# Low-rank adapters of a feed-forward layer in two groups of four sequences, with 256-column matmuls and high and low parts of a weight in one block

## The reference, cut to what matters

```python
H, F, RANK, SCALE = 1024, 2752, 16, 0.5
def lora_add(base, inp, A, B):              # A[16, RANK, in], B[16, out, RANK]
    Ab, Bb = A[lora_indices], B[lora_indices]      # one adapter for each sequence
    t = jnp.einsum('bri,bni->bnr', Ab, inp)
    return base + jnp.einsum('bor,bnr->bno', Bb, t) * SCALE
gate = lora_add(jnp.einsum('bnh,fh->bnf', x, W_gate), x, A_gate, B_gate)
up   = lora_add(jnp.einsum('bnh,fh->bnf', x, W_up),   x, A_up,   B_up)
act  = jax.nn.silu(gate) * up
x = x + lora_add(jnp.einsum('bnf,hf->bnh', act, W_down), act, A_down, B_down)
```

## Time and profile before

| | |
|---|---|
| time, median of 3 runs | 2395.77 us (2394.46 to 2396.67) |
| span of the profiled execution | 2393.5 us, from its first to its last instruction |
| what the median has beyond that span | 2.3 us |
| busy share of PE, PE's weight loads, DVE, ACT, POOL | 97%, 80%, 54%, 36%, 4% |
| granted TensorE clock, mean | 0.993 of full speed |
| start of L3 on PE | 701.7 us |
| DMA, mean rate | 172 GB/s; 352 to 354 in most of L1 and L2, 90 to 153 in L3 |

### The profile page before, as it was taken

One profiled execution on the slowest core, in us unless ns is written; L12 is line 12 of the kernel. 1 busy time (PEld: TensorE's weight loads), 2 busy tenths in 40 slices (PEclk: granted clock), 3 DMA queues, 4 the chain that ended last, 5 costly groups with the idle time before them and its releaser, 6 DMA issues.

```text
span 2393.5 us, 31068 instructions
## 1 busy us (share of the span) xinstructions
PE 2315.4 (97%) x10712; PEld 1915.5 (80%) x10712; DVE 1288.3 (54%) x1365; ACT 853.9 (36%) x775; POOL 101.6 (4%) x194
## 2 busy tenths in 40 slices
PE   2998999999989999999999999999999999999997
PEld 2997888788878888887888888788888878888885
DVE  7778999899974433443443345344334534433452
ACT  2214777677753321232332122233212223321221
POOL 4000000000000012000001200000020000000000
PEclk9999999999999999999999999999999999999999
DMA  6988999899953244333324433332442333232231
GB/s 218 337 324 317 353 352 353 307 354 352 352 203 99 97 136 153 99 107 115 99 95 137 153 99 107 115 99 93 139 153 99 107 115 99 90 118 79 99 107 65
DMA packets 127120, 412.42 MB, mean 172 GB/s; under 512 B 16918, under 2 KB 51926, under 8 KB 104918
## 3 DMA queue, kind: packets, MB, share of 16 engines
q1 hardware_dynamic: 115542, 379.32, 45.1%
q0 software_dynamic: 9344, 31.99, 4.1%
q10 hardware_dynamic: 2176, 0.26, 0.1%
HBM read 402.83 MB, written 32.28 MB: 182 GB/s over the span
## 4 chain that ended last, share of the span: by engine, by line
PE 93%; DVE 4%; issue 1%; DVEq 0%; ACT 0%; DMA 0%; POOL 0%; SPq 0%; ACTq 0%
PE ps L1145 24%; PE ps L1147 23%; PE ps L1146 23%; PE ps L1092 6%; PE ps L1094 6%; PE ps L1093 6%; PE ps L1069 3%; PE ps L1102 1%; DVE masked L743 1%; DVE red L702 0%; PE ps L1056 0%; DVE sin L659 0%; DVE mag L696 0%; DVE ang L659 0%; DVE turn L699 0%
## 5 line engine op out<-in xcount | busy, mean ns | idle before, releaser
L940 DVE TENSOR_TENSOR pl<-raw,ph 128x1152 fp32r<-128x1152 f32 (+2 forms) x240 | 343.1, 1430 | 919.0 <-ACT ph L559 919.0
L559 ACT ACTIVATE ph<-raw 128x1152 fp32r<-128x1152 f32 (+2 forms) x240 | 293.9, 1224 | 1172.0 <-PE ps L1147 1172.0
L1145 PE MATMUL ps<-xh,ph 128*128 128x512 f32 x1440 | 561.7, 390 | 8.1 <-DVE xl L958 7.3
L1146 PE MATMUL ps<-xl,ph 128*128 128x512 f32 x1440 | 561.3, 390 | 0.0
L1147 PE MATMUL ps<-xh,pl 128*128 128x512 f32 x1440 | 561.2, 390 | 0.0
L877 DVE TENSOR_TENSOR wl<-W,wh 128x2048 fp32r<-128x2048 f32 x160 | 362.3, 2286 | 29.0 <-ACT wh L501 29.0
L1145 PEld LDWEIGHTS ps<-xh,ph 128*128 128x128 f32 x1440 | 271.0, 188 | 65.6 <-DVE xl L958 7.5
L1147 PEld LDWEIGHTS ps<-xh,pl 128*128 128x128 f32 x1440 | 271.0, 188 | 56.4
L1146 PEld LDWEIGHTS ps<-xl,ph 128*128 128x128 f32 x1440 | 271.0, 188 | 56.2
L1145 PE MATMUL ps<-acth,ph 128*128 128x512 f32 (+1 forms) x792 | 312.5, 395 | 0.0
L1146 PE MATMUL ps<-actl,ph 128*128 128x512 f32 (+1 forms) x792 | 308.4, 389 | 0.0
(11 more groups left out here) (165 smaller groups left out, 1705.8 us busy)
## 6 DMA issues: line engine op xcount, KB each, us to landing
W<-in_w SPq DMA_DIRECT2D x160, 1024.0 KB, 4.9
raw<-in_wgu SPq DMA_DIRECT2D x168, 512.0 KB
toep<-kpad SPq DMA_DIRECT2D x32, 1024.0 KB, 8.1
raw<-in_wd SPq DMA_DIRECT2D x32, 768.0 KB
raw<-in_wd SPq DMA_DIRECT2D x32, 640.0 KB
picked_b<-in_lora_b POOLq DMA_DIRECT2D x32, 352.0 KB, 3.4
raw<-picked_b SPq DMA_DIRECT2D x168, 64.0 KB
urev<-in_urev SPq DMA_DIRECT2D x32, 256.0 KB, 4.1
```

The costliest lines, as they stand in the source:

```text
L559: nc.scalar.activation(ph[:, n % 2, 0:blocks * P], raw[:, n % RAW, 0:blocks * P], ACT.Copy).then_inc(hi_ready, 1)
L940: V.tensor_tensor(out=pl[:, n % 2, 0:blocks * P], in0=raw[:, n % RAW, 0:blocks * P], in1=ph[:, n % 2, 0:blocks * P].bitcast(F32), op=ALU.s ...
L1145: mm(bank(bk), lhsT=wh, rhs=mh, start=first, stop=False)
L1146: mm(bank(bk), lhsT=wh, rhs=ml, start=False, stop=False)
```

## The change

Eight sequences with one adapter block each become two groups of four (`GS` = 4 sequences, `GC` = 256 columns).

- Panels 0 and 1 are no longer gate and up, but group 0 and group 1: in each the rows 0 to 63 of the product are the gate adapters of four sequences and the rows 64 to 127 the up adapters. They run over the 256 columns of their group alone, 24 matmuls each.
- The second matrices take two blocks, one for each group, with the four adapters' 64 ranks in rows 0 to 63 and the same ranks again in rows 64 to 127. ACT rounds all 128 rows to high parts. DVE then puts the low part into rows 64 to 127. `tmh` holds the high part of the small product in both halves, `tml` its low part in rows 0 to 63 and zeros below. Two matmuls of 256 columns for each group (high and low weights x high, high weights x low) do what three of 512 columns did.
- The down adapter's first matrices (`AD0`, `AD1`): `ph` holds for each block of hidden channels the high parts of group 0 (64 columns) beside its low parts (64 columns), `pl` the same of group 1. For each block four matmuls of 256 columns take the place of three of 512. The high and low halves of the product are added later: ACT's `lift_adapter` copies one half down, DVE's `down_adapter` adds, masks and cuts.
- The eight last down panels: the half block of hidden channels (64 rows) and the down adapter's second matrices (64 ranks) share one block for each group. `wdh` holds the half block twice, and `gather` copies it beside the adapters. Nine full blocks are followed by six matmuls of 256 columns with 128 rows, where there were three with 64 rows and three with 128 rows, all of 512 columns.
- `gather` writes the second matrices twice (rows 0 to 63 and 64 to 127) in pieces of one rank, 512 bytes, where it wrote pieces of 8 KB. It issues six DMAs for each sequence and one more for each tile, where it issued five.

Counted in the same way, a tile now has 1536 matmuls of 512 columns and 360 of 256 columns: 48 in panels 0 and 1, 168 in the gate and up panels, 8 in the last one of them, 88 in `AD0` and `AD1`, 48 in the down panels. 294 matmuls of 512 columns are gone.

The diff, cut to its core:

```diff
+GS = TB // 2
+GC = GS * H
-GATHERED = TB * 5 * 16
+GATHERED = (TB * 6 + 1) * 16
@@ POOL, gather
+                    g, s = b // GS, b % GS
                     for k in range(2):
-                        pool.dma_start(lora_a[tile, k, :, b]...
+                        pool.dma_start(lora_a[tile, g, :, k, s]...
-                    pool.dma_start(lora_b[tile, :, b * R:(b + 1) * R].rearrange("t a r w -> (t a) (r w)"),
-                                   ins["lora_b"][one].rearrange("a n r w -> (a n) (r w)")).then_inc(lora_out, 16)
+                    for copy in range(2):
+                        r0 = copy * HALF + s * R
+                        pool.dma_start(lora_b[tile, :, r0:r0 + R, g].rearrange("t a r w -> (t a) r w"),
+                                       ins["lora_b"][one].rearrange("a n r w -> (a n) r w")).then_inc(lora_out, 16)
...
+                pool.dma_start(lora_bd[tile, :, 0:HALF].rearrange("t o r g w -> (t o) (r g w)"),
+                               ins["wdh"].rearrange("o r g w -> o (r g w)")).then_inc(lora_out, 16)
@@ ACT
+            def cut_down_adapter(n, blocks, t):
+                come(n, t)
+                for g, to in enumerate((ph, pl)):
+                    half = nc.scalar.activation(
+                        to[:, n % 2, 0:blocks * P].rearrange("p (k d s r) -> p d s k r", d=2, s=GS, r=R)[:, 0],
+                        raw[...][:, g * GS:(g + 1) * GS], ACT.Copy)
+                half.then_inc(hi_ready, 1)
+            def lift_adapter(t):
+                act.wait_ge(panel_done, t * NPAN + (AD1 + 3))
+                nc.scalar.activation(hid[0][HALF:P], bank(BANK_AD)[0:HALF], ACT.Copy).then_inc(lifted, 1)
...
-                        cut(4 + 2 * k, LT + 1, t, j)
+                        cut(4 + 2 * k, LT + 2, t, j)
@@ DVE
-            def cut(n, blocks, t, j=0):
+            def cut(n, blocks, t, j=0, lora=0):
...
+                if lora:
+                    ranks = slice(blocks * P, (blocks + lora) * P)
+                    main = V.tensor_tensor(out=ph[HALF:P, n % 2, ranks], in0=raw[HALF:P, n % RAW, ranks],
+                                           in1=ph[HALF:P, n % 2, ranks].bitcast(F32), op=ALU.subtract)
+                main.then_inc(lo_ready, 1)
...
+            def adapter(k, g, t):
...
+                V.tensor_tensor(out=part, in0=prod, in1=mask, op=ALU.mult)
+                for copy in range(2):
+                    last = V.tensor_tensor(out=tmh[copy * HALF:(copy + 1) * HALF, k, cols], in0=prod, in1=mask,
+                                           op=ALU.mult)
+                last.then_inc(th_ready, 1)
+                dve.wait_ge(th_ready, t * 7 + (count + 1))
+                V.tensor_tensor(out=tml[0:HALF, k, cols], in0=part, in1=tmh[own, k, cols].bitcast(F32),
+                                op=ALU.subtract).then_inc(t_ready, 1)
+            def down_adapter(t):
+                dve.wait_ge(lifted, t + 1)
...
@@ PE
+            def adapter(g, t):
+                panel_in(g, t)
+                cols = slice(g * GC, (g + 1) * GC)
+                for k in range(LT):
...
+                    last = three(ps[:, BANK_A - g, 0:GC], block_of(ph, g, k), block_of(pl, g, k),
+                                 xh[:, k, cols], xl[:, k, cols], k == 0, k == LT - 1)
+            def panel(n, bk, t, j=0, blocks=LT, at=0, start=True, ranks=(), ready=0):
...
+                for i, c in enumerate(ranks):
+                    for g in range(2):
+                        both = block_of(ph, n, blocks + 2 * i + g)
+                        to, cols = ps[:, bk, g * GC:(g + 1) * GC], slice(g * GC, (g + 1) * GC)
+                        mm(to, lhsT=both, rhs=tmh[:, c, cols], start=False, stop=False)
+                        last = mm(to, lhsT=both, rhs=tml[:, c, cols], start=False, ...)
+            def down_adapter(n, blocks, t, ready, start, stop):
+                panel_in(n, t)
+                for k in range(blocks):
+                    if k in ready:
+                        pe.wait_ge(act_ready, ready[k])
+                    for g, both in enumerate((ph, pl)):
...
+                        mm(to, lhsT=block_of(both, n, k), rhs=acth[:, k, cols], start=first, stop=False)
+                        last = mm(to, lhsT=block_of(both, n, k), rhs=actl[:, k, cols], start=False, stop=end)
+            def down(n, o, blocks, t, shared=False):
...
+                if shared:
+                    pe.wait_ge(t_ready, t * 5 + 5)
+                    for g in range(2):
+                        to, cols = ps[:, DOWN[o % 3], g * GC:(g + 1) * GC], slice(g * GC, (g + 1) * GC)
+                        last = three(to, block_of(ph, n, blocks + g), block_of(pl, n, blocks + g),
+                                     acth[:, blocks, cols], actl[:, blocks, cols], False, g == 1)
```

More of the change, by code:

```diff
@@ L368, in _ @@
                         sp.wait_ge(lora_out, ((t + 1) % NTILE + 1) * GATHERED)
-                    load(AD1 + 1 + o, lora_bd[bass.ds(t, 1), o].rearrange("t p w -> (t p) w"),
-                         at=F1 * P, incs=16)
+                    load(AD1 + 1 + o, lora_bd[bass.ds(t, 1), o].rearrange("t p g w -> (t p) (g w)"),
+                         at=(F1 - 1) * P, incs=16)
                 for k in range(2):
@@ L1035, in _ @@
                 cut(AD1 + 2, F1 + 1, t)
-                adapter(0, 2, AD1, BANK_AD, t)
+                down_adapter(t)
                 cut_rows((t + 1) % NTILE, t + 2)
@@ L1126, in _ @@
                 turn_product(base - 1, 1)
-            def panel(n, bk, blocks, hi, lo, t, j=0, start=True, stop=True, extra=(), extra_ready=0,
-                      ready=None, sem=act_ready, at=0):
-                pe.wait_ge(lo_ready, t * NPAN + j * 4 + (n + RAW + 1))
-                moving = [(hi[:, at + k], lo[:, at + k]) for k in range(blocks)]
-                moving += [(tmh[:, k], tml[:, k]) for k in extra]
-                for k, (mh, ml) in enumerate(moving):
-                    if extra and k == blocks:
-                        pe.wait_ge(t_ready, t * 3 + extra_ready)
-                    if ready and k in ready:
-                        pe.wait_ge(sem, ready[k])
-                    rows = HALF if hi is acth and n >= AD1 and k == F1 - 1 else P
-                    wh, wl, mh, ml = (a[0:rows] for a in (ph[:, n % 2, k * P:(k + 1) * P],
-                                                          pl[:, n % 2, k * P:(k + 1) * P], mh, ml))
-                    first, end = start and k == 0, stop and k == len(moving) - 1
-                    mm(bank(bk), lhsT=wh, rhs=mh, start=first, stop=False)
-                    mm(bank(bk), lhsT=wh, rhs=ml, start=False, stop=False)
-                    last = mm(bank(bk), lhsT=wl, rhs=mh, start=False, stop=end)
@@ new lines, in panel @@
+            def panel(n, bk, t, j=0, blocks=LT, at=0, start=True, ranks=(), ready=0):
+                panel_in(n, t, j)
+                for k in range(blocks):
+                    last = three(bank(bk), block_of(ph, n, k), block_of(pl, n, k), xh[:, at + k], xl[:, at + k],
+                                 start and k == 0, False)
+                if ranks:
+                    pe.wait_ge(t_ready, t * 5 + ready)
+                for i, c in enumerate(ranks):
[3 more added lines that the diff above has]
+                        mm(to, lhsT=both, rhs=tmh[:, c, cols], start=False, stop=False)
+                        last = mm(to, lhsT=both, rhs=tml[:, c, cols], start=False,
+                                  stop=c == ranks[-1] and g == 1)
@@ L1163, in _ @@
                 done = lambda k: t * FT + (k + 1)
-                panel(AD0, BANK_AD, F0, acth, actl, t, stop=False,
-                      ready={0: done(F0 - 3), F0 - 2: done(F0 - 2), F0 - 1: done(F0 - 1)})
+                down_adapter(AD0, F0, t, {0: done(F0 - 3), F0 - 2: done(F0 - 2), F0 - 1: done(F0 - 1)},
+                             start=True, stop=False)
                 for o in range(LT):
-                    panel(AD0 + 1 + o, DOWN[o % 3], F0, acth, actl, t)
+                    down(AD0 + 1 + o, o, F0, t)
                 with pe.Fori(0, F1 // 2 - 1) as j:
@@ L1171, in _ @@
                 gate_up(0, AD1 - 4, t)
[L1172 to L1176 removed]
+                panel(AD1 - 2, GATE[1], t, blocks=LT // 2)
+                panel(AD1 - 1, GATE[1], t, blocks=LT // 2, at=LT // 2, start=False, ranks=(0, 1), ready=4)
+                down_adapter(AD1, F1, t, {0: done(FT - 3), F1 - 2: done(FT - 2), F1 - 1: done(FT - 1)},
+                             start=False, stop=True)
                 for o in range(LT):
[L1178 to L1179 removed]
+                    down(AD1 + 1 + o, o, F1 - 1, t, shared=True)
 def kernel(**inputs):
```

160 lines of the change are left out of this document (99 added, 61 removed).

## The result

| | median us | lowest to highest | runs |
|---|---|---|---|
| before | 2395.6 | 2394.5 to 2396.7 | 4 |
| after | 2318.3 | 2317.0 to 2319.3 | 4 |

The ratio is 0.9676 (95% interval 0.9664 to 0.9688). The kernel is faster by 77.3 us. 100.8 us were forecast, so 23.5 us are missing.

A forecast was written before the change was run, and what follows sets the result against it. PE's matmul count times start distance was taken to bound L3. Per tile 25.6 + 3.8 - 3.7, times four 102.8, less 2 for the gather: 100.8 us gained, 2295 us forecast, range 2278 to 2335.

The forecast's parts named there:

- the forecast's own share: Whole kernel: the chance of 0.69 given to the forecast itself, counted from 2280 to 2316 us.
- rival C: Waits at short panels twice as long, 512-byte gather pieces at half rate holding up the convolution: 2320 us; chance 0.13.
- main term: L3 on PE: 294 matmuls of 512 columns go, 360 of 256 come, gaining 25.6 us per tile.
- half block: Eight down panels and AD1: no more switching to 64 rows and back, 0.42 us each, gaining 3.8 us per tile.
- I take 0.114: Distance between 256-column matmuls in L3, about half the measured 0.2267 us; 360 of them make 41.0 us.
- upper of the two near bounds: 256-column distance of 0.120 us, if 0.0134 came once per matmul; the whole kernel would be 9 us up.
- floor of 0.109: Lower bound for the 256-column distance, from 128-column transposes with weight loads, eight in 0.87 us.
- those rows lie on the floor: Argument against partly hidden weight loads (distance 0.13 to 0.17, 2318 to 2376 us, chance 0.10), citing plain float32 short matmuls.
- Rival A: Weight loads not hidden by 256-column matmuls: 0.222 us each, some 2437 us in all, slower by 41; chance 0.07.
- I leave it out: Start of AD1: DVE's extra operation in the cut before, some 0.4 us, was given no cost.
- the convolution's own loads can be late by nothing (they are asked for ahead): Lower end of the gather's delay to the convolution, up to 4 us; 2 us was taken, once.
- six of eight sequences are issued by 40 us: Tile 0's gather: only the other quarter and `wdh`, some 4 us, would fall between 40 and 80 us.

The follow-up runs named there:

- experiment 1: The kernel before, with only the half block's three matmuls in AD1 and the last down panels given 128 rows instead of 64: 2381.1 us, ratio 0.9939.
- Experiment 2: The changed kernel, with tile 0's gather spread out: three sequences at the start, five and the half block during L1 and L2: 2317.6 us, ratio 0.9670.
- experiment 7: The changed kernel, with tile 0's copies of the down adapter's matrices and `wdh` made at the start of L3: 2312.2 us, ratio 0.9652.
- experiment 8: The changed kernel with four edits: half block earlier, panel 2's adapter steps first, `hidden` before the next cut, down-panel gather deferred: 2299.8 us, ratio 0.9598, fastest version run.

## Why the prediction was right in sign and 23 us too low

The time is inside the range of 2278 to 2335, at 2318.3, but 2 us above the 2316 up to which the forecast's own share was counted, and near the 2320 of rival C. That rival had the waits grow by 15 us in all and the gather cost 10 us more. Less than half of that came: 4 us more of waits and 6 more for the gather; 3 us at the tile boundaries are in neither. The largest part of what is missing is the spacing of matmuls. The main term's mechanism and the half block held; four terms fell short.

**Spacing of 256-column matmuls: right mechanism, mis-sized by 8%.** "I take 0.114" was the step. Measured, they are 0.118 to 0.120 apart, and the 512-column matmuls behind them in each panel lose another 0.026 in all. For the 360 of a tile that makes 0.1228 each and 360 x 0.0088 = 3.2 us per tile more than forecast. The upper of the two near bounds, 0.0134 us per matmul on top of one column per cycle, was the right reading at 256 columns: it gives 0.120. (At 128 it would give 0.067, where three of four distances are 0.110 to 0.113.) Half of a measured distance halves that fixed part too. The floor of 0.109 was also not the lowest row on record. The convolution's plain float32 matmuls of 32 to 96 columns follow one another at 0.085 and 0.112 in turn, and those of 256 columns at 0.215, so "those rows lie on the floor" holds for the transposes alone. The formula of the Trainium skill (TensorE: Matmul & The Clock Gate, Back-to-back issue gap), 109 ns, lies 10 ns below the measured 119, as it lay 11 below at 512 columns.

Rival A is refuted: the loads are recorded at 188 ns and the matmuls follow at 119, all with full rows. The Trainium skill (TensorE: Matmul & The Clock Gate, What overlaps and what doesn't) says that a load overlaps matmuls in flight only where the row group differs. The rows here go against it, before and after.

**The half block: right.** 14.3 us alone (experiment 1), 15 forecast. The 0.8 us between them are about what the three boundaries took back there (1.2 us).

**Waits in L3: forecast 3.7 us per tile, measured 4.7.** With the slow distance behind each:

| place | forecast | measured |
|---|---|---|
| panel 2 | 0.40 | 0.46 |
| panel 3 | 0.05 | 0.76 |
| last block of `AD0` | 1.10 | 1.01 |
| start of `AD1` | 0 | 0.62 |
| last block of `AD1` | 1.75 | 1.10 |
| first down panel after `AD1` | 0.40 | 0.65 |
| start of the last gate and up panel before `AD1` | 0 | 0.11 |

The places were found, two were sized wrong. The prediction had three adapter steps of DVE take 4.35 us before panel 3's cut. From the kernel after:
```profile
1116.16 0.42 DVE L972 TENSOR_TENSOR ph<-raw,ph 64x256 fp32r<-64x256 f32 x1
...
1121.62 1.21 DVE L968 TENSOR_TENSOR pl<-raw,ph 128x1024 fp32r<-128x1024 f32 x1
...
1123.32 0.50 PE L1196 MATMUL ps<-xh,ph 128*128 128x512 f32 x1 [0.48 <-DVE ph L972]
```
They run from 1116.61 to 1121.62, 5.0 us, 1.67 each and not 1.45. A margin of 0.05 us was one rounding away from a wait, and should have been written as such. At `AD1`, "I leave it out" was the step that failed: the start is 0.52 us late. DVE works without a gap from 1440.27 until 1445.91, when the last cut for `AD1` ends, and PE was through with the panel before at 1445.52. The extra operation in the cut before (L972 at 1440.98) takes 0.69 us of this, more than the "some 0.4" put down for it. No run took it out alone. That later start, and the longer spacing, in turn shorten the wait at its last block from 1.75 to 0.99 us.

**The tile boundary: missed, 1.1 us per tile.** The prediction had no term for the "issue" ahead of a tile, which was 0.9 us over the whole of L3. Behind it stood a branch of 4.5 us of which matmuls covered 4.15. Shorter matmuls at a tile's end took part of the cover away, also where the half block became ordinary (experiment 1). The prediction never asked what covers this item and what it costs without the cover.

Together per tile 3.2 + 1.0 + 1.1 = 5.3 us, where tile 1 fell short by 5.2. Over the whole, spacing makes 12.7 us, waits 4.0, three boundaries 3.4 and the gather 5.6, less the 2.3 of luck in the last store: 23.4, where the spans fell short by 22.8.

**The gather: forecast 2 us, measured 7.6.** Two steps failed. First, "the convolution's own loads can be late by nothing (they are asked for ahead)". They are asked for ahead, but not far enough. The first `toep` load reads what `kpad` has just received, and the chain of the kernel after shows `kpad`, `toep` and the matmuls in a row. The load issued at 66.95 us took 14.7 us, and PE came for it 3.7 us before it had landed. Second, "six of eight sequences are issued by 40 us": POOL was behind. Each issue of the gate and up matrices, now in pieces of 512 bytes, took 0.90 instead of 0.53 us, and there are 16 instead of 8 for tile 0. Five of eight sequences had begun by 40 us (six before), and the last issue ended at 75 us instead of 57, in the stretch where the DMA share is 1.00. Of these 18 us the longer issues make 10; the rest are gaps between issues, up to 8.1 us, that the profile calls "issue". "Some 4 us" of bytes at full share was the bound that I gave. The result is above it (L1's first matmul starts at 217.0 instead of 208.3, where the prediction had "at most 4 us later"), and 2.4 us of it are PE's seventh set at 1.2 GHz. Experiment 2 shows that moving the copies into L1 and L2 does not lower the price, and experiment 7 that what is first needed at `AD0`, near 860 us, costs less at the start of L3. How the rest splits between bytes, issues and pieces stays open. L3's start also moved between the five kernels that differ only behind it (707.7 to 712.7 in single profiles, mean 710.6), where the kernel before and experiment 1 have 701.7 and 701.8. So by these profiles the gather cost 6 to 11 us, and 7.6 is no exact figure. With experiment 7's edit it is 705.6, and 707.0 in experiment 8.

## What to carry to other kernels

Cost a matmul of half the length as its columns plus a fixed part taken from the row of the long one, not as half of the long one's distance, and add something for the change of length. Look for the row of the shortest dense matmuls too, since below it the columns no longer count. When the bounding engine gets faster over some stretch, go through the operations of the feeding engines in their order there: an operation that is due now, behind a cut that has time, costs nothing to swap, and here such swaps at the start of a tile and at both down adapters gave 12 of the 18 us that the last version gained. An item that the profile calls "issue" can be covered work like any other; ask what covers it before you shorten that. Here it was the branch back over a long loop body.

## What the runs showed of the hardware

- PE's branch back over the whole body of the loop over tiles takes 4.46 to 5.25 us and is taken up 17 matmuls ahead of the array, in all ten kernels. Its branches back in short loops take 0.21 to 0.23. ACT's and DVE's records of the branch over tiles take 0.05. Only the long ones have an instruction transfer of 16 KB inside. With 17 matmuls of 512 columns the branch shows as 1.0 to 1.8 us between two matmuls, with 11 of 512 and 6 of 256 as 1.6 to 2.0.
- Going to 64 rows of weights and back costs 0.42 us for the block of three matmuls, with nothing else changed.
- float32r matmuls with a weight load each: 0.2267 us apart at 512 columns, 0.118 to 0.120 at 256, 0.110 to 0.113 at 128 but for the first of a run (0.058). Behind 128-column ones the first of 512 loses 0.05 us more.
- Plain float32 matmuls in the convolution, a weight load each: 0.215 us apart at 256 columns, 0.110 at 128, 0.085 and 0.112 in turn at 96 and below.
- Behind each wait of PE in tile 1, the first matmul stands 0.10 to 0.11 us further from the second than in the stream.
